# Pair products moved to the end of their own head's step, the selections and the first and last inverse re-placed, in a one-core decoder layer

## The reference

```
attention: q, k, v = silu(causal_conv4(x @ Wq, Wk, Wv)), 8 heads of 128, two k and two v per token
  q, k l2-normalised; beta = 2 sigmoid(x @ Wb); g = -exp(A_log) softplus(x @ Wa + dt_bias)
  per token:  state *= exp(g);  for j in 0, 1:  u = (v_j - k_j . state) beta_j;  state += k_j u
              o = q . state
  out = (rmsnorm(o) * norm_w * silu(x @ Wg)) @ Wo
cross attention: similarities of 64 context features (256 x 256 a batch); for each row the 76 largest kept;
  mixed symmetrically by gamma with the normalised rows
feed-forward: top-2 of 8 experts plus a shared one, 704 wide, silu(g) * u
```

## Time and profile before

| | |
|---|---|
| median of 3 runs | 943.59 us (938.92 to 947.09) |
| profiled execution, its own time | 940.37 us |
| its span | 938.3 us |
| PE, DVE, ACT, POOL busy | 89%, 56%, 42%, 37% of the span |
| steps 0 to 10 (attention) | first 632 us |
| feed-forward | from there to the end |

### The profile page before, as it was taken

The page is one execution under the profiler, slowest core; times in us unless marked ns, Lnnn a source line. Parts: engine busy times, 40 slices in busy tenths (PEclk is TensorE's granted clock), DMA queues, the critical chain, the costliest instruction groups (busy, mean ns, idle before and its releaser), DMA issues.

```text
span 938.3 us, 16243 instructions
## 1 busy us (share of the span) xinstructions
PE 835.7 (89%) x5560; PEld 580.5 (62%) x5561; DVE 530.1 (56%) x1285; ACT 390.9 (42%) x839; POOL 347.5 (37%) x654
## 2 busy tenths in 40 slices
PE   3969999989999999899899876874999999999992
PEld 2343566756766756767667765663667667666761
DVE  4564757878878868878778755465511111111113
ACT  3536756545654554655555323202222222222220
POOL 0157368457456565563683580003330000000015
PEclk9788999999999999999999886897999999999997
DMA  7302230130031031021201301009563100110104
GB/s 204 78 12 56 69 85 1 24 80 12 13 80 23 7 74 22 14 68 24 51 1 24 83 9 29 1 1 384 215 228 129 34 28 28 34 34 22 34 25 127
DMA packets 102593, 57.88 MB, mean 62 GB/s; under 512 B 64192, under 2 KB 98048, under 8 KB 102528
## 3 DMA queue, kind: packets, MB, share of 16 engines
q1 hardware_dynamic: 99488, 51.62, 20.0%
q0 software_dynamic: 1536, 4.20, 1.4%
q10 hardware_dynamic: 1504, 1.20, 0.4%
HBM read 42.45 MB, written 14.55 MB: 61 GB/s over the span
## 4 chain that ended last, share of the span: by engine, by line
PE 72%; DVE 10%; ACT 5%; POOL 4%; issue 4%; DMA 3%; SPq 1%; ACTq 0%; POOLq 0%; DVEq 0%
PE bank L1599 16%; PE bank L582 11%; PE bank L1644 9%; PE bank L712 3%; PE bank L590 3%; PE bank L637 3%; DVE y L1055 3%; PE bank L746 2%; PE bank L716 2%; PE bank L711 2%; PE bank L697 2%; PE bank L1631 2%; PE bank L596 2%; PE bank L671 2%; PE bank L683 2%
## 5 line engine op out<-in xcount | busy, mean ns | idle before, releaser
L1055 DVE SCALAR_TENSOR_TENSOR y<-bank,cwh,y 128x510 f32<-128x510 f32 (+2 forms) x240 | 177.5, 743 | 82.5 <-ACT y L833 78.8
L582 PE MATMUL bank<-xnT,wbuf 128*128 128x512 f32 x320 | 164.8, 641 | 5.5 <-DVE y L1055 5.0
L1599 PE MATMUL bank<-f_wgu,f_xgT 128*128 x368 | 118.8, 466 | 0.0
L1858 DVE TENSOR_TENSOR f_act<-f_sg,bank 128x352 f32<-128x352 f32 x62 | 32.2, 521 | 139.8 <-PE bank L1599 135.1
L1370 POOL TENSOR_TENSOR term<-inv,blk 128x126 f32<-128x126 f32 (+22 forms) x248 | 87.4, 352 | 63.3 <-DMA blk<-a_blocks 44.5
L1933 POOL DMA_INDIRECT f_back<-slots_y,f_slot x16 | 15.4, 960 | 228.8 <-DMA slots_y<-f_yb 222.2
L582 PEld LDWEIGHTS bank<-xnT,wbuf 128*128 128x128 f32 x320 | 56.8, 197 | 67.4 <-issue 53.8
L1373 POOL TENSOR_TENSOR inv<-inv,term 128x126 f32<-128x126 f32 (+22 forms) x248 | 91.2, 368 | 19.4
L1706 ACT ACTIVATE f_sg<-bank 128x352 f32<-128x352 f32 x62 | 28.6, 463 | 158.7 <-PE bank L1599 158.7
L1644 PE MATMUL bank<-f_wdn,f_actT 128*128 (+1 forms) x372 | 91.5, 387 | 0.8 <-ACT f_actT L1719 0.8
L1599 PEld LDWEIGHTS bank<-f_wgu,f_xgT 128*128 128x128 f32 x368 | 66.2, 190 | 36.8 <-issue 7.6
(11 more groups left out here) (204 smaller groups left out, 1501.4 us busy)
## 6 DMA issues: line engine op xcount, KB each, us to landing
f_wgu<-in_exp_gu SPq DMA_DIRECT2D x8, 1408.0 KB, 8.7
f_wdn<-in_exp_dn SPq DMA_DIRECT2D x8, 640.0 KB, 9.3
blk<-a_blocks SPq DMA_DIRECT2D x16, 256.0 KB, 3.9
slots_x<-oT SPq DMA_DIRECT2D x24, 128.0 KB, 1.9
f_xg<-slots_x SPq DMA_DIRECT2D x24, 128.0 KB, 2.0
slots_y<-f_yb SPq DMA_DIRECT2D x23, 128.0 KB, 1.7
a_blocks<-aT SPq DMA_DIRECT2D x64, 32.0 KB, 1.6
inverses<-inv SPq DMA_DIRECT2D x16, 128.0 KB, 3.0
```

The lines of the kernel that those rows point to most:

```text
L582: last = mm(bankA[p % 2][:, :], wbuf[A.par][:, kt, wblk, :], xnT[:, kt, (p % 2) * 512:(p % 2 + 1) * 512], start=kt == 0, stop=kt == 1)
L1055: v.scalar_tensor_tensor(out=y[p % 2][:, :, k:], in0=src[:, :, 0:SEQ - k], scalar=cwh[A.par][:, cb, 3 - k:4 - k], in1=y[p % 2][:, :, k:], ...
L1599: last = mm(gu[c][:, 0:FFH], xt[:, k, :], wgu[:, e, k, at:at + FFH], start=k == 0, stop=k == 1)
L1858: v.tensor_tensor(av[:, par, half * FFH:(half + 1) * FFH], sg[:, half, :], gu[2 * half + 1][:, 0:FFH], ALU.mult).then_inc(f_act, 1)
```

## The change

The pair items move from stage B, ahead of slot 0, to stage A of the same head, into slot 11 and `LAST` of the step before. In `LAST` they stand between the level items. The tables of steps 0, 1 and 8 are different: in steps 1 and 8 the levels stand behind everything else. The second half of `p64` and the first half of `t64` are issued as alternating products (`joined`). `aT` is doubled, `mq` has three buffers, and POOL writes the masked decay straight into `mq`. `gather` stands at the end of SP's step. The squares and their sums are done earlier, in pairs, and `norm_sum` with `fold_beta` stands in slot 8 rather than 10. `ex` moves from slot 0 to 1 and the third `kend` from 11 to 9. The selection is split 10, 4 and 6 instructions over slot 0, slot 3 and behind `LAST`, where it was 8 in slot 0 and 12 in slot 11; in step 8 the second tile's 20 follow behind `LAST`. POOL prepares the next head's decay input (`start`) and identity (`unit`) right behind the decays.

```diff
-FIRST, LAST = "first", "last"
-FILL = {FIRST: {"B": [("pair", n) for n in range(BC // 2)]},
-        0: {"A": [("dx", 0), ("dx", 1), ("ex", 0), ("ex", 1)]},
-        1: {"E": [("out", 0)], "B": [("vtok", 0)]},
+LAST = "last"
+FILL = {0: {"A": [("dx", 0), ("dx", 1)]},
+        1: {"A": [("ex", 0), ("ex", 1)], "E": [("out", 0)], "B": [("vtok", 0)]},
         2: {"B": [("vtok", 1)]},
         3: {"B": [("vtok", 2)]},
         4: {"E": [("out", 1)]},
@@ -112,13 +111,25 @@
         6: {"B": [("kend", 0)]},
         7: {"E": [("out", 2)]},
         8: {"B": [("kend", 1)]},
-        9: {"B": [("gate", 0)]},
+        9: {"B": [("gate", 0), ("kend", 2)]},
         10: {"B": [("p32", 0), ("p32", 1)], "E": [("out", 3)]},
-        11: {"B": [("t32", 0), ("t32", 1), ("kend", 2)]},
-        LAST: {"B": [("x32", 0), ("x32", 1), ("gate", 1), ("p64", 0), ("p64", 1), ("t64", 0), ("t64", 1)]}}
-PLACES = [FIRST] + list(range(12)) + [LAST]
+        11: {"B": [("t32", 0), ("t32", 1)], "A": [("pair", 0), ("pair", 1)]},
+        LAST: [("B", [("x32", 0)]), ("A", [("pair", 2), ("pair", 3)]), ("B", [("x32", 1)]), ("A", [("pair", 4)]), ("B", [("p64", 0), ("gate", 1)]),
+               ("B", [("p64", 1), ("t64", 0)]), ("A", [("pair", 5), ("pair", 6), ("pair", 7)]), ("B", [("t64", 1)])]}
+LEVELS = [("p32", 0), ("p32", 1), ("gate", 1), ("t32", 0), ("t32", 1), ("x32", 0), ("x32", 1), ("p64", 0), ("p64", 1), ("t64", 0), ("t64", 1)]
+JOIN = {("p64", 1): ("t64", 0)}
+
+STEP_0 = {0: {}, 1: {}, 3: {"A": [("dx", 0), ("dx", 1), ("ex", 0), ("ex", 1)]}}
+STEP_1 = {10: {},
+          11: {"A": [("pair", 0), ("pair", 1), ("pair", 2), ("pair", 3)]},
+          LAST: [("A", [("pair", 4), ("pair", 5), ("pair", 6), ("pair", 7)]), ("B", LEVELS)]}
+STEP_8 = {10: {"E": [("out", 3)]},
+          11: {},
+          LAST: [("B", LEVELS)]}
+PLACES = list(range(12)) + [LAST]
 LAG = {"A": 0, "B": 1, "C": 2, "E": 3}
 B_BANKS = 3
+TOP_PARTS = {0: (0, 10), 3: (10, 14), LAST: (14, 2 * ROUNDS)}
 
 
 FIRST_DECAYS = 3
@@ -128,8 +139,12 @@
 
     table = FILL[place]
     if step == 0:
-        table = FILL[0] if place == FIRST_DECAYS else {} if place == 0 else table
-    return table.items()
+        table = STEP_0.get(place, table)
+    if step == 1:
+        table = STEP_1.get(place, table)
+    if step == HEADS:
+        table = STEP_8.get(place, table)
+    return table.items() if isinstance(table, dict) else table
...
-    dm = sb("dm", [P, BC, STEPS])
+    mq.append(sb("mq2", [P, BATCH, CH, STEPS]))
...
-        def gather(B):
+        def gather(A):
 
             for u in range(2):
-                sp.wait_ge(at_done, 8 * B.h + 4 * u + 4)
+                sp.wait_ge(at_done, 8 * A.h + 4 * u + 4)
                 for q in range(BLOCKS):
                     rows_ = slice(q * NB, (q + 1) * NB)
-                    sp.dma_start(diag[q][:, 8 * u:8 * u + 8, :], aT[rows_, 2 * u:2 * u + 2, :, rows_].rearrange("p b c n -> p (b c) n")).then_inc(a_out, 16)
-            sp.wait_ge(a_out, 32 * BLOCKS * (B.h + 1))
+                    sp.dma_start(diag[q][:, 8 * u:8 * u + 8, :], aT[A.par][rows_, 2 * u:2 * u + 2, :, rows_].rearrange("p b c n -> p (b c) n")).then_inc(a_out, 16)
+            sp.wait_ge(a_out, 32 * BLOCKS * (A.h + 1))
             for k in range(2):
                 sp.dma_start(blk[k * STEPS:(k + 1) * STEPS, :, :].rearrange("p r i -> p (r i)"), blocks).then_inc(blk_in, 16)
...
         def step(A, B, C, E):
-            if B:
-                gather(B)
...
                 scatter(B)
             if s == 1:
                 tiles_out()
+            if A:
+                gather(A)
+            if s == 1:
+                sp.wait_ge(sim_out, 64)
                 tile_in(0)
...
+        def joined(first, second, X):
+            banks = [bankB[bank_of(kind, X.h, n)] for kind, n in (first, second)]
+            for kind, n in (first, second):
+                bank_free(pe, kind, X.h, n)
+                level_ready(kind, n, X.h)
+            for k in range(BC // 2):
+                one_, two_ = level(*first, X, k, banks[0]), level(*second, X, k, banks[1])
+            one_.then_inc(b_mm, 1)
+            two_.then_inc(b_mm, 1)
...
-                    last = mm(out, U[:, b, :], mq[par][:, b, c, :], start=c == 0, stop=True)
+                    last = mm(out, U[:, b, :], mq[h % 3][:, b, c, :], start=c == 0, stop=True)
...
-                if A and 6 <= slot < 10:
-                    norm(A, slot - 6)
                 if s == 0 and slot == 0:
                     gate_logits()
                 if A and slot < 10:
                     proj(A, slot)
+                if A and slot in (5, 7):
+                    norm(A, slot - 5)
+                    norm(A, slot - 4)
...
-                if A and 5 <= slot <= 10:
-                    square(A, slot - 5)
+                if A and slot in (4, 6, 8):
+                    square(A, slot - 4)
+                    square(A, slot - 3)
                 if A and slot < 10:
                     evac(A, slot)
-            fill(LAST)
             if C:
                 out_square(C, A.h if A else HEADS - 1)
+            fill(LAST)
...
-                if n == 0 and B.h >= 2:
-                    dve.wait_ge(o_mm, 4 * (B.h - 1) + 1)
-                v.tensor_tensor(mq[B.par][:, b, cs, :], both[:, :, MU:MU + STEPS], dm[:, 2 * n:2 * n + 2, :], ALU.mult).then_inc(qk_used, 1)
+                keep = mq[B.h % 3][:, b, cs, :]
+                v.tensor_tensor(keep, both[:, :, MU:MU + STEPS], keep, ALU.mult).then_inc(qk_used, 1)
...
-                if tiles and slot == 0:
-                    topk(tiles[0], 0, 8)
-                if not A and tiles and slot == 5:
-                    topk(tiles[0], 8, 2 * ROUNDS)
-                if not A and tiles and slot == 9:
+                if tiles and slot in TOP_PARTS:
+                    topk(tiles[0], *TOP_PARTS[slot])
+                if s == HEADS and slot == 9:
                     gamma_parts()
-                    topk(tiles[1], 0, 2 * ROUNDS)
                 if s == HEADS + 1 and slot < TT_N:
                     mix_mask(slot)
                 if s == HEADS + 1 and 3 <= slot < 3 + TT_N:
                     mix_add(slot - 3)
-                if B and slot == 9:
+                if B and slot == 9 and 1 < s < HEADS:
                     turn_blocks(B)
-                if A and slot == 10:
+                if A and slot == 8:
                     norm_sum(A, 0)
                     fold_beta(A)
                 if A and slot == 11:
-                    if tiles:
-                        topk(tiles[0], 8, 2 * ROUNDS)
                     norm_sum(A, 1)
             fill(LAST)
+            if B and s in (1, HEADS):
+                turn_blocks(B)
             if C:
                 out_gate(C)
+            if tiles:
+                topk(tiles[0], *TOP_PARTS[LAST])
+                for n in tiles[1:]:
+                    topk(n, 0, 2 * ROUNDS)
...
-            if B:
-                clear(B)
-                unit(B)
-            if A:
-                start(A)
             if E:
                 out_rms(E)
             if B:
                 invert(B)
             if A:
                 if A.h == 0:
+                    start(A)
+                    unit(A)
                     pool.wait_ge(scal_done, 4)
                     g.tensor_scalar(scal[:, :, 0, :], scal[:, :, 0, :], -1.0, None, ALU.mult).then_inc(scal_done, 1)
                     pool.wait_ge(scal_done, 5)
                 decays(A)
+                if A.h + 1 < HEADS:
+                    start(Head(A.h + 1, (A.h + 1) % 2, (A.h + 1) // 2))
+                if A.h:
+                    unit(A)
                 fold_beta(A)
                 norm(A)
                 scalars(A)
                 q_decay(A)
+                clear(A)
```

67 lines of the change are left out of this document (37 added, 30 removed).

## The result

The changed kernel takes 958.75 us in the median of 4 runs (953.27 to 965.76), the kernel before 943.57 (938.92 to 947.09): a ratio of 1.016, 95% interval 1.011 to 1.022. The prediction was 937.6 us with a range of 916 to 951, so it had the wrong sign: it forecast 6 us less, and 15 us more were measured. The profiled execution took 959.65 us (span 957.5), 19.3 us more than the one of before. Ratios here leave out executions far above the fastest of their kernel, medians don't, so one can't be divided out of the other.

What follows compares the result with a forecast made beforehand. PE was taken to bound full steps, a chain of waits the stretch around step 8. Six full steps +6, steps 0 to 2 -4, steps 7 to 9 -8 sum to -6: median 943.6 to 937.6 us, range 916 to 951.

Steps and rivals of the forecast that it cites:

- The rival with a chance of 0.12: DVE becomes the bound, PE's clock falls, up to 3 us a step beyond the sum; 960 us, chance 0.12.
- my sum of +1.0: Full step, 2 to 7: -1.6 + 0.2 - 0.1 + 1.3 + 1.2 = +1.0 us; six steps +6.
- steps 0 to 2: Start of the kernel: the wait for `gm` goes, most of the lead is given back; -4 us, from -9 to +2.
- steps 7 to 9: Row sums of step 8 to slot 2 of step 9: selections leave the scan; -8 us, from -12 to -2.
- Middle, slots 8 to 10: Full step: DVE gets `norm_sum` and `kend` scaling ahead of `turn_blocks`, so the levels of slot 10 wait +1.2 us.
- The clock: PE's clock in full steps: no term in the sum, only a rival's case, at up to 3 us a step.
- Middle, slot 5: Full step: four selection instructions behind slot 3 make PE wait +1.3 us at slot 5.
- Head: Start of a full step: PE waits about 2 us for DVE at slot 2; head takes 10.3 us, -0.1.
- Tail: Slot 11 and the new `LAST` of a full step: 15.8 us against 17.4, -1.6, plus 0.2 for shape changes.
- The joined level: Tail: 32 alternating 64 x 64 instructions take 1.05 us instead of 2.08, a gain of 1.0.
- The bank wait of 0.6 at pair 4: Tail: `pair 4` takes the bank of `pair 2`, which DVE reaches only after the queries' `norm_sum`; 0.6 us of waiting.
- Rival 1: Fillers deliver: DVE's chain overlaps better, PE stays the bound, a full step saves 2 to 3.4 us; 917 us, chance 0.30.

Runs made afterwards that it cites:

- transpose first: Changed kernel with the transpose of the inverse issued on DVE right behind the scan's part of slot 9: 948.67 us, 1.000 of before.
- three edits: Changed kernel with the transpose right behind the scan in slot 9, selection in DVE's gaps, and second gate product ahead of the first 32 x 32 level: 914.10 us.
- selection, gate ahead: Changed kernel with selection in DVE's gaps and the second gate product ahead of the first 32 x 32 level, transpose left late: 919.63 us.
- both: Changed kernel with the transpose right behind the scan in slot 9 and the selection in DVE's gaps: 927.74 us, ratio 0.981.
- `kend` back: Changed kernel with transpose right behind the scan in slot 9 and selection in DVE's gaps, plus the third `kend` returned to slot 11: 925.73 us.

## Why the prediction was wrong, step by step

The rival with a chance of 0.12 came true, at 958.75 against its 960. Its mechanism was right: DVE is late, and PE's clock falls behind the wait. It priced that at up to 3 us a step beyond my sum of +1.0, and the step became 4.3 longer. But it named slot 2 as the place, and the place is slot 10; and that the number fits so well is luck, since its terms for the ends missed by 4.4 one way (steps 0 to 2) and 2.9 the other (steps 7 to 9).

Of the 3.3 us a step by which my sum fell short, 2.9 are the clock, which the sum put at nothing, and 1.2 the wait at the first level, which it had too short; the other terms give 0.8 back.

- **Middle, slots 8 to 10: the first step that failed.** I put +1.2 there and measured 2.36 of waiting. (The terms as I wrote them, 1.84 and 0.7 less 0.6 and 0.5, give 1.4; 0.4 of slack ahead of the old level was left out.) DVE's side came nearly as added up: 1.84 and 0.7 less 0.6 of gaps, and the chain is 2.0 longer. PE's side was wrong. I let the moved `kend` product hold PE back by 0.5 and left another part of the diff uncosted: the two groups of `norm` products of slots 8 and 9 (0.36 us each) went to slots 5 and 7. PE reaches the level 10.8 us after slot 8 begins (378.35 to 389.11), which is 0.5 earlier than before (363.36 to 374.61, 11.25), not 0.5 later. This is read from the rows; no run puts these products or `norm_sum` back.
- **The clock: the second, and the dearer.** My sum has no term for it. I took it for a matter of a rival, since the earlier trace rows showed it at the head of the step, where the waits were 1.1 and 1.3. That slow stretch of 1.7 us went; a dearer one came, 1.5 to 4.5 us, behind the wait at the first level. Two runs tie it to this wait: one of 2.5 us put there costs 5.7 us beyond itself in three of five steps of the kernel before, and a gate product put there in the changed one takes the slow stretch behind the level out of all five steps, against a short one at slot 5 in two. What makes it dear is its length: 3.4 us at the lower level cost 1.7 at the head of a step and 1.5 here, 10.2 us cost 4.5. Whether it is longer here because small products follow is not shown.
- **Middle, slot 5.** +1.3 against 1.11, for the `U` of slot 4 (line 1203): right. The 0.37 for `R` in slot 4 stood in the kernel before too (346.97).
- **Head.** 2 us of waiting at slot 2 against 0.95, for DVE as said; the head takes 10.0 us, not 10.3. DVE's chain takes 10.4 us (410.68 to 421.07) against the 10.5 added up, but it begins 0.4 ahead of the row sums, and PE has 9.1 us of work beside it (411.10 to 420.17), where I had put 8.3.
- **Tail.** 15.8 + 0.2 against 16.80 in step 5, of which 0.8 is slow clock in slot 11: right at full clock. The joined level took 1.07 as predicted, but the gain was 0.75, since two levels one behind the other take 1.82 and not 2.08. The bank wait of 0.6 at pair 4 did not come: the scaling of the queries' sums, which I priced at the 1.53 that it took before, took 0.17 (400.94), and why it got shorter is not shown. I saw no effect of the changes of shape beyond tenths of a microsecond.
- **Steps 7 to 9.** -8 against -7.9; the first level 44.2 us after the row sums against 45.5 (the terms that I wrote give 44.9). The run with the old step 8 shows a gain once more (9.9). But the size hangs on the clock, and that it fits is in part luck: with the step 8 of before, the stretch of 71.9 us took 73.5 in the second trace and only 65.1 (560.65 to 625.71) in the kernel with a wait put in, where the clock came back earlier (second 32 x 32 level in 1.20 us, not 1.92). With the new step 8 it takes 59.9 to 65.4 in twelve traces.
- **Steps 0 to 2: a third miss.** -4 against +1.4 at slot 2 of step 2 (141.35 less 139.95). No wait for `gm`, the pairs wait 4.87, the decay products come at 131.78: each about as predicted, the last 0.8 beyond the late end. A wait of 2.14 for the transpose at the levels (116.34) stood in no term, and neither did the clock: the view by stretches has it at 0.74 from 100 to 120 us and 0.66 from 120 to 140, where the kernel before has 1.00 and 0.91. The difference of single traces says little here: the kernels with this step 0 and 1 reach that point at 133.7 to 134 in four traces and at 139 to 143 in the others, with the clock of the early stretches (0.91 of full speed between 20 and 40 us in the changed kernel, 1.00 in the one with the transpose first), and the kernel before at 135.4 and 140.0. Put side by side by that clock: at 1.00 the four come at 133.7 to 133.9 and the kernel before at 135.4; at 0.91 the changed kernel at 141.4 (and four others of its order at 139.5 to 141.9) and the kernel before with a wait, whose steps 0 and 1 are those of before, at 137.5; at 0.66 the second trace of the changed kernel at 142.8 and before at 140.0. So a gain of 1.6 stands against losses of 2 to 4. With the old step 1 that point comes at 139.9 with the clock at 1.00 up to 60 us, 6 us behind those four, so the new step 1 is better within the new order.

Rival 1, that the fillers deliver 2 to 3.4 a step, was right on what the order can give with DVE's work placed anew, and wrong on what it gives as it stands: with three edits a full step takes 63.0 us, 3.7 less than before, and the kernel 914.1.

**What stays open.** A wait of PE near the first level can bring the lower clock, and the gate product ahead of it mostly keeps it up there. What exactly decides isn't settled: 1.2 was followed by a slow stretch twice (selection, gate ahead), 1.14 was not in one trace (both) and 1.13 was in another (`kend` back); 0.33 with 0.86 behind it was in two steps of five (transpose first), and in the kernel with both edits in one of two, for a short stretch. The clock also has a history: the long steps alternate with short ones where the waits are the same.
